# Head layout of three sixteen-head attention stages: copies within SBUF in place of a trip through DRAM

## The chip, the cores and the metric

The kernel runs on one core of a Trainium2 chip. The metric is the device time of one execution in microseconds. Three executions took 2805.46, 2811.95 and 2813.29 us (median 2811.95). The traces and tables show one further, profiled execution, which took 2811.11 us; its span from the first to the last instruction is 2809.3 us.

## The reference

A decoder of eleven stages works on 8 sequences of 256 tokens with 256 channels (2048 tokens), with a context of 120 tokens a sequence. Four stages are attention with 16 heads of 16 channels. For each of them the reference is, in short:

```
q = (x @ Wq + bq), k = (source @ Wk + bk), v = (source @ Wv + bv)   # 256 channels = 16 heads of 16
p = softmax(q_h . k_h / 4 + mask)        # for each head h
x = layernorm(x + concat_h(p @ v_h) @ Wo + bo)
```

L0a attends over tokens mixed across sequences, L1a is causal with rotary embedding, L1x attends over the context (120 keys a sequence), L2a is causal with keys and values from a latent of 64 channels. The other seven stages (cross attention, experts, product keys, feed-forward) are not touched.

## The kernel before, in words

Activations lie transposed in SBUF, channels on the 128 partitions, tokens along the row. The stages run one after the other, and each is built from blocks. A block ends in a barrier over all engines, so that nothing of the next block starts before the slowest engine of this one is through; the wait that SP (SyncE) makes at the end of its program counts as well.

`heads_stage` builds the four sixteen-head stages (L0a, L1a, L1x, L2a). Its first block projects. TensorE makes Q in four chunks of 512 tokens, two halves of 128 channels each, ScalarE copies each half from PSUM to `Qc` (L1118), then TensorE makes K in chunks (four of 512; in L1x two of 480) and VectorE copies these to `Kc` (L1142), then V (L1098, L1150). `Qc` and `Kc` are compact: head h lies on 16 rows starting at 16(h mod 8), in half h div 8. The score matmuls of the next block want each head at the start of a 32-row group: the padded tiles `Q` and `K` have four groups of rows (head mod 4, rows 32i to 32i+15) by four planes (head div 4), and the other 16 rows of a group hold a constant that GpSimd (L1033) and VectorE (L1123) write beforehand.

Moving the heads from compact to padded is SP's work in this first block. For each chunk `put_heads` stores it to DRAM in one transfer over all 128 partitions (L980, 512 KB), and `take_heads` waits until that store has landed and loads it back in four transfers of 128 KB, each into 16 rows by four planes (L992). The store of a chunk is issued ahead of the loads of the chunk before it; the two semaphores `put0` and `put1` take turns. After the last chunk SP waits for all loads (L1013, L1014; in L0a also L1016) and only then reaches the barrier. L1a, with rotation, has a store in two transfers instead of one (L977) and is otherwise alike.

The second block computes scores for the row maximum, the third scores again, exponentials and values. There the results go from padded back to compact rows by copies within SBUF, 16 rows by 512 tokens and 32 KB each in L0a and L1x (L1310, half of them issued by SP, half by ScalarE's queue). These are the only copies of that kind in the kernel before.

Of the kernel before, what the change touches and what calls it, by code (L numbers as in the profile page):

```python
# [18 lines left out]
P = 128  # L19
# [3 lines left out]
DH = D // P  # L23
# [109 lines left out]
NCH = T // CH  # L133
# [780 lines left out]
HD, HEADS, HP, G4 = 16, 16, 32, 4  # L914


def heads_stage(nc, c, name):

    a = HEADS16[name]
    s, w, ps = c.sig, c.w[name], c.psum  # L920
    kv, keys, mix, rope = a["kv"], a["keys"], a.get("mix"), a.get("rope")
# [5 lines left out]
    KCH, KCHN = (B * CTX // 2, 2) if ctx_keys else (CH, NCH)  # L927
# [4 lines left out]
    with ExitStack() as ctx:  # L932
        def sb(nm, shape, dt=F32, where=ctx):
            return where.enter_context(nc.sbuf_tensor(f"{name}_{nm}", shape, dt))

        Q = sb("Q", [P, G4, T])
        K = sb("K", [P, G4, B * KTOK])
# [6 lines left out]
        def padded_rows(h):  # L944
            return slice(HP * (h % 4), HP * (h % 4) + HD)

        def compact_rows(h):
            return slice(HD * (h % 8), HD * (h % 8) + HD)

        with ExitStack() as part:  # L950
            lat = sb("lat", [P, 1, T], F32, part) if kv == "lat" else None
            R = sb("R", [P, 2, DH, CH], F32, part) if rope else None
            Qc = sb("Qc", [P, DH, T], F32, part)
            Kc = sb("Kc", [P, DH, B * KTOK], F32, part)
# [5 lines left out]
            items = [("q", n, CH) for n in range(NCH)], [("k", n, KCH) for n in range(KCHN)]  # L960
            if rope:
                items = [x for pair in zip(*items) for x in pair]
            else:
                items = items[0] + items[1]

            PUTS = 16 * DH if rope else 16

            def put_heads(sp, slot, kind, n, width):
                cols = slice(n * width, (n + 1) * width)
                if rope:  # L970
                    sp.wait_ge(s["rope_add"].sem, s["rope_add"].at(2 * n + (1 if kind == "q" else 2)))
                else:
                    sp.wait_ge(s[f"{kind}_evac"].sem, s[f"{kind}_evac"].at(DH * (n + 1)))
                whole = Qc if kind == "q" else Kc
                if rope:
                    for j in range(DH):
                        sp.dma_start(c.heads[kind][:, cols].rearrange("(h j i) t -> j h i t", j=DH, i=HD // 2)[j],  # L977
                                     whole[:, j, cols]).then_inc(s[f"put{slot}"].sem, 16)
                else:
                    sp.dma_start(c.heads[kind][:, cols].rearrange("(j p) t -> p j t", p=P), whole[:, :, cols])\  # L980
                        .then_inc(s[f"put{slot}"].sem, 16)

            def take_heads(sp, slot, turn, kind, n, width):
                cols = slice(n * width, (n + 1) * width)
                sp.wait_ge(s[f"put{slot}"].sem, s[f"put{slot}"].at(PUTS * turn))
                if kind == "q":
                    sp.wait_ge(s["q_clear"].sem, s["q_clear"].at(n // 2 + 1))
                else:
                    sp.wait_ge(s["k_clear"].sem, s["k_clear"].at(1))
                stored = c.heads[kind][:, cols].rearrange("(g i d) t -> i d g t", i=4, d=HD)  # L990
                for i in range(4):
                    sp.dma_start((Q if kind == "q" else K)[padded_rows(i), :, cols], stored[i]).then_inc(s[f"laid_{kind}"].sem, 16)  # L992

            with nc.Block() as block:  # L994
                @block.sync
                def _(sp):

                    if mix:
                        own = c.ins["xpT"].rearrange("(j p) t -> p j t", p=P)
                        c.load_first(sp)  # L1000
                        sp.dma_start(xp[:, :, 0:CH], own[:, :, 0:CH]).then_inc(s["tile0"].sem, 16)
                        c.load(sp, 0, PACK[name][0]["bk"][0])
                        for n in range(1, NCH):
                            sp.dma_start(xp[:, :, n * CH:(n + 1) * CH], own[:, :, n * CH:(n + 1) * CH]).then_inc(s[f"tile{n}"].sem, 16)
                        c.load_base(sp)
                    c.prefetch(sp, name)
                    for i, item in enumerate(items):
                        put_heads(sp, i % 2, *item)
                        if i:
                            take_heads(sp, (i - 1) % 2, (i + 1) // 2, *items[i - 1])  # L1010
                    i = len(items) - 1
                    take_heads(sp, i % 2, i // 2 + 1, *items[i])
                    sp.wait_ge(s["laid_q"].sem, s["laid_q"].at(64 * NCH))  # L1013
                    sp.wait_ge(s["laid_k"].sem, s["laid_k"].at(64 * KCHN))  # L1014
                    if mix:
                        sp.wait_ge(c.loaded.sem, 16 * 4)  # L1016

# [140 lines left out]
            counts = dict(v_proj=B * VT, v_evac=B * VT, w_first=16 if mix else 0, padded_v=1, q_clear=2, k_clear=1)  # L1158
            if mix:
                counts.update({f"tile{n}": 16 for n in range(NCH)})  # L1160
            counts.update(laid_q=64 * NCH, laid_k=64 * KCHN, put0=PUTS * ((len(items) + 1) // 2), put1=PUTS * (len(items) // 2))
            if rope:
                counts.update(rope_proj=2 * NCH, rope_mul=2 * NCH, rope_add=2 * NCH)
            else:
# [130 lines left out]
        with ExitStack() as part:  # L1295
# [4 lines left out]
            width = 3 * P if keys == "causal" else CH  # L1300
# [2207 lines left out]
def program(nc, ins, out):  # L3508
    c = Core()
    with ExitStack() as ctx:  # L3510
# [106 lines left out]
        for name in run:  # L3617
            if name in HEADS16:
                heads_stage(nc, c, name)
            elif name in ATTENTION:  # L3620
                attention_stage(nc, c, name)
            else:
                OTHER[name](nc, c, ins)
# [132 lines left out]
```

## Time and profile before

| | |
|---|---|
| median of three runs | 2811.95 us |
| profiled execution | 2811.11 us, span 2809.3 us |
| TensorE matmul busy | 2139.6 us (76%) |
| VectorE busy | 1704.1 us (61%) |
| ScalarE busy | 955.7 us (34%) |
| GpSimd busy | 850.2 us (30%) |
| first block of L0a | 0 to 68 us |
| first block of L1x | 850 to 894 us |
| first block of L2a | 1333 to 1395 us |

A busy share over the whole span says little here, since the eleven stages have different limits. What counts for a change to one block is which engine or queue of that block reaches the barrier last, and how long the others have then been idle. The granted clock of TensorE averages 0.877 of full speed.

### The profile page before, as it was taken

Reading aid. Unit: us, or ns where it says so; the run is one execution under the profiler, and the core shown is the slowest. Engines: PE = TensorE matmul, PEld = TensorE weight load, DVE = VectorE, ACT = ScalarE, POOL = GpSimd, SP = SyncE. Lnnn points to the kernel's source line nnn. Section 1 sums busy time; section 2 is a strip of 40 time slices with the busy share of each in tenths; the row PEclk is TensorE's granted clock in tenths of the full one; section 3 lists DMA queues with packets and bytes.
Section 4 is the critical chain, followed back from the end, with each engine's and each line's share of the span. In section 5 each row is a group of like instructions: output and inputs, shape, how many; then the busy total and the mean of one; then the engine's idle time right before and its main releaser. Section 6 shows DMA issues by size and latency. Waiting matters only on the chain. (4 is left out here: it accounts for less than half of the span.)

```text
span 2809.3 us, 37739 instructions
## 1 busy us (share of the span) xinstructions
PE 2139.6 (76%) x13417; PEld 1415.7 (50%) x13417; DVE 1704.1 (61%) x4445; ACT 955.7 (34%) x1774; POOL 850.2 (30%) x807
## 2 busy tenths in 40 slices
PE   6887679876887775684679685778787788668796
PEld 3544459834543442572355333666676666535332
DVE  3754411176654768445485676678888877536586
ACT  0142324310351331232105464344454444335343
POOL 1001032250001007451100002777777777303000
PEclk8999679988998876897799898888898988889898
DMA  8210057437007134653601204422222222130000
GB/s 232 67 26 3 25 186 264 141 93 198 13 20 182 51 125 162 215 187 134 120 2 28 78 1 126 109 60 65 59 61 61 59 67 62 41 88 1 0 0 30
DMA packets 133770, 241.88 MB, mean 86 GB/s; under 512 B 41824, under 2 KB 78816, under 8 KB 127080
## 3 DMA queue, kind: packets, MB, share of 16 engines
q1 hardware_dynamic: 69887, 128.53, 15.9%
q0 software_dynamic: 56416, 102.76, 11.8%
q10 hardware_dynamic: 7296, 8.40, 1.0%
q8 instruction: 97, 1.59, 0.2%
q14 instruction: 74, 0.60, 0.1%
HBM read 267.00 MB, written 69.73 MB: 120 GB/s over the span
## 5 line engine op out<-in xcount | busy, mean ns | idle before, releaser
L3000 POOL DMA_INDIRECT L2f_G<-in_L2f_table,L2f_idx x512 | 530.2, 1036 | 174.2 <-issue 153.6
L3351 DVE CUSTOM_DVE_ANT_0 L2f_junk<-L2f_G,L2f_X 128x256 bf16<-128x256 f32 x512 | 182.7, 421 | 131.8 <-DMA L2f_G<-in_L2f_table,L2f_idx 131.5
L3075 PE MATMUL psum<-L2f_G,L2f_diag 128*128 128x256 f32 x768 | 188.2, 397 | 0.0
L3075 PEld LDWEIGHTS psum<-L2f_G,L2f_diag 128*128 128x128 f32 x768 | 152.0, 201 | 34.2 <-issue 7.3
L1192 PE MATMUL psum<-constb 128*128 128x256 bf16 x512 | 91.4, 284 | 74.7 <-PEq L994 39.8
L3052 PE MATMUL psum<-xT,L2f_mw 128*128 128x256 f32 x512 | 135.2, 412 | 11.9 <-DVE L2f_h L3357 11.9
L2350 POOL DMA_INDIRECT picks_x<-L1f_rows,L1f_put x64 | 71.3, 1114 | 207.4 <-DVE L1f_sm L2563 188.2
L3215 ACT ACTIVATE L2f_diag<-const,L2f_actd 128x128 f32<-128x128 f32 x400 | 123.9, 389 | 29.9 <-DVE L2f_actd L3365 29.9
L3052 PEld LDWEIGHTS psum<-xT,L2f_mw 128*128 128x128 f32 x512 | 106.7, 210 | 30.9 <-DVE L2f_h L3357 13.1
L3208 ACT ACTIVATE L2f_actd<-L2f_dots 128x9 f32<-128x9 f32 (+1 forms) x64 | 13.5, 210 | 285.6 <-DVE L2f_dots L3351 285.6
L1192 PEld LDWEIGHTS psum<-constb 128*128 128x128 bf16 x512 | 40.8, 99 | 131.3 <-issue 59.9
L3062 PE MATMUL psum<-L2f_h,L2f_mw 128*128 128x256 f32 x256 | 74.5, 418 | 41.4 <-DVE L2f_acc L3401 41.4
L1371 ACT ACTIVATE L1a_PT<-psum 128x1536 f32<-128x1536 f32 x32 | 46.4, 1451 | 169.8 <-PE psum L1341 169.8
L1719 ACT ACTIVATE L0f_h<-psum,L0f_wu 128x128 f32<-128x128 f32 x184 | 57.6, 364 | 97.6 <-PE psum L1693 97.6
L1693 PEld LDWEIGHTS psum<-L0f_xeT,L0f_wu 128*128 128x128 f32 x736 | 88.3, 197 | 2.1 <-issue 1.0
L1693 PE MATMUL psum<-L0f_xeT,L0f_wu 128*128 128x128 f32 x736 | 88.5, 280 | 0.6 <-DVE L0f_xeT L1727 0.6
L2704 POOL DMA_INDIRECT picks_y<-L1f_ye,L1f_home x64 | 62.0, 969 | 73.6 <-ACT L1f_ye L2769 61.0
L1705 PE MATMUL psum<-L0f_wd,L0f_h 128*128 128x256 f32 x368 | 83.2, 379 | 0.0
L1862 PE MATMUL psum<-L3f_h,weights 128*128 128x512 f32 x128 | 65.6, 660 | 22.4 <-DVE L3f_h L1933 22.4
L2124 POOL TENSOR_TENSOR L2x_room<-L2x_Fu 128x256 f32<-128x256 f32 x8 | 5.6, 722 | 253.8 <-ACT L2x_Fu L2134 253.7
L3062 PEld LDWEIGHTS psum<-L2f_h,L2f_mw 128*128 128x128 f32 x256 | 53.0, 210 | 52.2 <-issue 44.3
L1705 PEld LDWEIGHTS psum<-L0f_wd,L0f_h 128*128 128x128 f32 x368 | 68.1, 190 | 8.3
(671 smaller groups left out, 5036.4 us busy)
## 6 DMA issues: line engine op xcount, KB each, us to landing
L1f_we<-in_L1f_w SPq DMA_DIRECT2D x32, 384.0 KB, 9.7
picks_x<-zeros SPq DMA_DIRECT2D x16, 544.0 KB, 8.7
L1f_xe<-picks_x SPq DMA_DIRECT2D x32, 272.0 KB, 2.8
picks_y<-zeros SPq DMA_DIRECT2D x16, 512.0 KB, 6.5
L2f_G<-in_L2f_table,L2f_idx POOLq DMA_INDIRECT x512, 2.8
slots_x<-zeros POOLq DMA_DIRECT2D x8, 512.0 KB, 7.6
L1f_wb<-in_L2x_w SPq DMA_DIRECT2D x1, 4096.0 KB, 12.1
L1f_g<-picks_y SPq DMA_DIRECT2D x8, 512.0 KB, 13.1
```

The costliest lines, as they stand in the source:

```text
L1192: nc.tensor.matmul(out, c.one, m.broadcast_to([P, 2, P]), start=True, stop=False, skip_group_check=True)
L1693: mm = nc.tensor.matmul(ps[:, f // 2, (f % 2) * TILE:(f % 2 + 1) * TILE], wu[:, k, j * F + f * P:j * F + f * P + P], xeT[:, k, j, :], star ...
L1705: mm = nc.tensor.matmul(ps[:, 6 + k, 0:D], h[:, k, f, :], wd[:, k, f * D:(f + 1) * D], start=(f == 0), stop=(f == FT - 1))
L1862: mm = nc.tensor.matmul(ps[:, 4 + 2 * (n % 2) + o, :], w["w2"][:, f * D + o * P:f * D + o * P + P], h[:, u % 2, i * CH:(i + 1) * CH], star ...
L2350: nc.gpsimd.indirect_dma_start(out=c.picks_x[:, :], out_offset=bass.IndirectOffsetOnAxis(ap=put[:, t, k:k + 1], axis=0), in_=rows[:, t, :] ...
L2704: nc.gpsimd.indirect_dma_start(out=c.picks_y[:, :], out_offset=bass.IndirectOffsetOnAxis(ap=home[:, e % NB, q:q + 1], axis=0), in_=ye[:, e ...
L3000: nc.gpsimd.indirect_dma_start(out=G[:, h, k, :], out_offset=None, in_=ins["L2f_table"], in_offset=bass.IndirectOffsetOnAxis(ap=IDX[:, t, ...
L3052: mm = nc.tensor.matmul(ps[:, UP + i % 2, chunk(g)], wt[:, j * F + f * P:j * F + f * P + P], c.xT[:, j, chunk(k)], start=(j == 0), stop=(j ...
L3062: mm = nc.tensor.matmul(ps[:, DOWN, chunk(o_)], wd[:, f * D + o_ * P:f * D + o_ * P + P], h_[:, i % 3, :], start=(f == 0 and o_ == 0), sto ...
L3075: mm = nc.tensor.matmul(ps[:, MIX + t % 2, 0:D], diag[:, i % 2, k, :], row[:, D:2 * D], start=(h == 0 and k == 0), stop=(h == HEADS - 1 an ...
L3215: e = nc.scalar.activation(diag[:, i % 2, k, :], c.ident, ACT.Copy, scale=act_d[:, i % 2, k:k + 1])
L3351: e = VE.tensor_tensor_reduce(out=junk[:, k, :], in0=row[:, 0:D], in1=X[:, t % 3, :], scale=1.0, scalar=0.0, op0=ALU.mult, op1=ALU.add, ac ...
```

## The change

In the stages without rotation (L0a, L1x, L2a) the store to DRAM and the four loads of a chunk are replaced by eight transfers straight from the compact tile to the padded one. For each i of 0 to 3 and each parity 16 rows of `Qc` by two halves by 512 tokens go to rows 32i of `Q`, in planes 0 and 2 or in planes 1 and 3: 32 pieces of 2 KB, 64 KB a transfer. The wait for the store's semaphore is gone; the waits for the copies out of PSUM and for the cleared padding stay, and stand ahead of the eight transfers. The counts at the end of the block follow (128 a chunk instead of 64). L1a is as before.

```diff
+            LAID = 64 if rope else 128
+            PUTS = 16 * DH if rope else 0
+
+            def lay_heads(sp, kind, n, width):
+                cols = slice(n * width, (n + 1) * width)
+                whole, padded = (Qc, Q) if kind == "q" else (Kc, K)
+                if kind == "q":
+                    sp.wait_ge(s["q_clear"].sem, s["q_clear"].at(n // 2 + 1))
+                else:
+                    sp.wait_ge(s["k_clear"].sem, s["k_clear"].at(1))
+                sp.wait_ge(s[f"{kind}_evac"].sem, s[f"{kind}_evac"].at(DH * (n + 1)))
+                for i in range(4):
+                    for odd in range(2):
+                        sp.dma_start(padded[padded_rows(i), odd::2, cols], whole[compact_rows(4 * odd + i), :, cols])\
+                            .then_inc(s[f"laid_{kind}"].sem, 16)
...
-                    for i, item in enumerate(items):
-                        put_heads(sp, i % 2, *item)
-                        if i:
-                            take_heads(sp, (i - 1) % 2, (i + 1) // 2, *items[i - 1])
-                    i = len(items) - 1
-                    take_heads(sp, i % 2, i // 2 + 1, *items[i])
-                    sp.wait_ge(s["laid_q"].sem, s["laid_q"].at(64 * NCH))
-                    sp.wait_ge(s["laid_k"].sem, s["laid_k"].at(64 * KCHN))
+                    if rope:
+                        for i, item in enumerate(items):
+                            put_heads(sp, i % 2, *item)
+                            if i:
+                                take_heads(sp, (i - 1) % 2, (i + 1) // 2, *items[i - 1])
+                        i = len(items) - 1
+                        take_heads(sp, i % 2, i // 2 + 1, *items[i])
+                    else:
+                        for item in items:
+                            lay_heads(sp, *item)
+                    sp.wait_ge(s["laid_q"].sem, s["laid_q"].at(LAID * NCH))
+                    sp.wait_ge(s["laid_k"].sem, s["laid_k"].at(LAID * KCHN))
```

SP's program in the first block of L0a, before: from the last load of weights to the third chunk of Q. L980 is the store, L992 the loads, and a row with "waits" names the semaphores ahead of it.

```order
L3553 DMA weights<-in_w_L0x 128x1796
L980 DMA heads_q<-L0a_Qc 128x2x512 [waits q_evac] x2
L992 DMA L0a_Q<-heads_q 16x4x512 [waits q_clear,put0]
L992 DMA L0a_Q<-heads_q 16x4x512 x3
L980 DMA heads_q<-L0a_Qc 128x2x512 [waits q_evac]
L992 DMA L0a_Q<-heads_q 16x4x512 [waits q_clear,put1]
L992 DMA L0a_Q<-heads_q 16x4x512 x3
```

The same place after the change (L979 is the new copy, L3564 the load of weights):

```order
L3564 DMA weights<-in_w_L0x 128x1796
L979 DMA L0a_Q<-L0a_Qc 16x2x512 [waits q_evac,q_clear]
L979 DMA L0a_Q<-L0a_Qc 16x2x512 x7
L979 DMA L0a_Q<-L0a_Qc 16x2x512 [waits q_evac,q_clear]
L979 DMA L0a_Q<-L0a_Qc 16x2x512 x7
L979 DMA L0a_Q<-L0a_Qc 16x2x512 [waits q_evac,q_clear]
```

Five transfers and two kinds of wait for each chunk have become eight transfers behind one wait, and no transfer waits for another any more.

The end of SP's program in the first block of L2a, before, with the last two chunks of K and the wait that leads to the barrier:

```order
L992 DMA L2a_K<-heads_k 16x4x512 x3
L980 DMA heads_k<-L2a_Kc 128x2x512 [waits k_evac]
L992 DMA L2a_K<-heads_k 16x4x512 [waits k_clear,put0]
L992 DMA L2a_K<-heads_k 16x4x512 x3
L992 DMA L2a_K<-heads_k 16x4x512 [waits k_clear,put1]
L992 DMA L2a_K<-heads_k 16x4x512 x3
L994 UNCONDITIONAL_BRANCH [waits laid_k,laid_q]
```

And after:

```order
L979 DMA L2a_K<-L2a_Kc 16x2x512 [waits k_evac,k_clear]
L979 DMA L2a_K<-L2a_Kc 16x2x512 x7
L979 DMA L2a_K<-L2a_Kc 16x2x512 [waits k_evac,k_clear]
L979 DMA L2a_K<-L2a_Kc 16x2x512 x7
L1001 UNCONDITIONAL_BRANCH [waits laid_k,laid_q]
```

The last store and the wait for it have left the end of the block; sixteen copies stand where one store and eight loads stood. The other engines' programs keep their order.

## Rows read from the trace of the kernel before

**Rows 1.** The page's first line.

```profile
span 2809.3 us, 37739 instructions
```

**Rows 2.** Timeline around the end of L0a's first block: start, duration, engine, line.

```profile
50.55 0.42 DVE L1150 TENSOR_TENSOR L0a_V<-psum,weights 128x256 f32<-128x256 f32 x1 [0.44 <-PE psum L1098]
...
67.98 1.87 PE L1195 MATMUL psum<-constb 128*128 128x512 bf16 x4 [17.47 <-PEq L994]
```

**Rows 3.** The same around the end of L1x's first block.

```profile
886.19 0.16 DVE L247 TENSOR_TENSOR weights<-weights,L1x_mid 128x2 f32<-128x2 f32 x1
...
893.98 1.43 PE L1251 MATMUL psum<-L1x_K,L1x_Q 32*128 32x120 f32 x18 [10.27 <-PEq L994]
```

**Rows 4.** The same for L2a.

```profile
1372.71 0.16 DVE L247 TENSOR_TENSOR weights<-weights,L2a_mid 128x2 f32<-128x2 f32 x1
...
1395.00 1.01 PE L1192 MATMUL psum<-constb 128*128 128x256 bf16 x4 [24.77 <-PEq L994]
```

**Rows 5.** SP's queue: what it waited for at the three block ends (L0a, L1x, L2a).

```profile
SPq L1016 <- DMA L0a_K<-heads_k: 5.4, 1, 5.4
...
SPq L1014 <- DMA L1x_K<-heads_k: 6.5, 1, 6.5
...
SPq L1014 <- DMA L2a_K<-heads_k: 6.4, 1, 6.4
```

**Rows 6.** SP's queue in L2a: first stores, and loads of the last chunks of K.

```profile
1346.91 3.80 SPq L980 DMA_DIRECT2D heads_q<-L2a_Qc  x2
...
1370.71 1.72 SPq L992 DMA_DIRECT2D L2a_K<-heads_k  x4
...
1375.96 1.71 SPq L992 DMA_DIRECT2D L2a_K<-heads_k  x4
...
1386.39 1.71 SPq L992 DMA_DIRECT2D L2a_K<-heads_k  x4
```

**Rows 7.** SP's queue in L0a: first stores, first loads, last loads.

```profile
13.60 3.62 SPq L980 DMA_DIRECT2D heads_q<-L0a_Qc  x2
26.16 1.74 SPq L992 DMA_DIRECT2D L0a_Q<-heads_q  x4
...
60.36 1.71 SPq L992 DMA_DIRECT2D L0a_K<-heads_k  x4
```

**Rows 8.** SP's queue in L1x: first stores, first loads, last loads.

```profile
856.43 3.80 SPq L980 DMA_DIRECT2D heads_q<-L1x_Qc  x2
...
860.34 2.22 SPq L992 DMA_DIRECT2D L1x_Q<-heads_q  x4
...
884.91 1.71 SPq L992 DMA_DIRECT2D L1x_K<-heads_k  x4
```

**Rows 9.** Windows: busy time by engine, TensorE clock, DMA share, GB/s.

```profile
1346.90:1350.50 3.60, 3.60 (x10) 1.67 (x9) 0.00 (x0) 1.38 (x2) 0.00 (x0) 1.00 0.38 146
...
1368.00:1378.00 10.00, 2.23 (x11) 1.61 (x9) 4.69 (x12) 0.00 (x0) 0.00 (x0) 0.74 1.06 210
...
13.00:26.00 13.00, 13.00 (x32) 5.82 (x31) 0.75 (x1) 4.70 (x7) 0.19 (x1) 1.00 1.02 411
```

**Rows 10.** Copies within SBUF, L1x: issue ns, time to landing, one window with four.

```profile
L1310 SPq DMA_DIRECT2D L1x_ATc<-L1x_Q x32: 507/586/962, 955.6 to 999.6; - x32
...
DMA to landing us min/median/max: 1.9/2.2/2.7
...
958.00:961.00 3.00, 2.79 (x33) 1.37 (x32) 2.15 (x5) 1.88 (x1) 0.00 (x0) 1.00 0.21 44
```

**Rows 11.** Copies out of PSUM: ns min/median/max, first and last start.

```profile
L1118 ACT ACTIVATE L2a_Qc<-psum,weights x8: 688/688/688, 1344.5 to 1356.5; 128x512 f32<-128x512 f32 x8
...
L1142 DVE TENSOR_SCALAR L0a_Kc<-psum,weights x8: 751/751/751, 24.8 to 36.7; 128x512 f32<-128x512 f32 x8
L1142 DVE TENSOR_SCALAR L2a_Kc<-psum,weights x8: 750/750/751, 1357.4 to 1363.4; 128x512 f32<-128x512 f32 x8
```

**Rows 12.** GB/s in 40 slices of 1381 to 1394, the last loads of L2a.

```profile
GB/s 177 183 151 189 246 189 170 120 113 183 303 347 290 202 107 76 76 69 63 113 240 164 139 114 120 113 120 126 126 88 76 63 57 82 95 50 19 0 0 0
```

**Rows 13.** Issues of the loads of Q in L1x: ns of one issue, min/median/max.

```profile
L992 SPq DMA_DIRECT2D L1x_Q<-heads_q x16: 302/426/821, 860.3 to 875.5; - x16
```

More of the change, by code:

```diff
@@ L964, in heads_stage @@
                 items = items[0] + items[1]
-            PUTS = 16 * DH if rope else 16
+            LAID = 64 if rope else 128
[12 more added lines that the diff above has]
+                            .then_inc(s[f"laid_{kind}"].sem, 16)
             def put_heads(sp, slot, kind, n, width):
                 cols = slice(n * width, (n + 1) * width)
[L970 to L973, printed above, removed]
+                sp.wait_ge(s["rope_add"].sem, s["rope_add"].at(2 * n + (1 if kind == "q" else 2)))
                 whole = Qc if kind == "q" else Kc
[L975 to L981, printed above, removed]
+                for j in range(DH):
+                    sp.dma_start(c.heads[kind][:, cols].rearrange("(h j i) t -> j h i t", j=DH, i=HD // 2)[j],
+                                 whole[:, j, cols]).then_inc(s[f"put{slot}"].sem, 16)
             def take_heads(sp, slot, turn, kind, n, width):
@@ L1160, in heads_stage @@
                 counts.update({f"tile{n}": 16 for n in range(NCH)})
-            counts.update(laid_q=64 * NCH, laid_k=64 * KCHN, put0=PUTS * ((len(items) + 1) // 2), put1=PUTS * (len(items) // 2))
+            counts.update(laid_q=LAID * NCH, laid_k=LAID * KCHN, put0=PUTS * ((len(items) + 1) // 2), put1=PUTS * (len(items) // 2))
             if rope:
```

## The prediction, made before the changed kernel was timed

> **What bounds the kernel now.** The page's first line gives the scale: a span of 2809.3 us inside an execution of 2811.11 us, so 1.8 us lie outside the span [rows 1]. Shares of busy time over the whole program say nothing about this edit, so I read the timeline at the three block ends that it touches. In L0a the last compute instruction, a copy of V out of PSUM, ends at 50.97, and the first matmul of the next block starts at 67.98 [rows 2]. In L1x VectorE ends at 886.35 and the next matmul starts at 893.98 [rows 3]; in L2a 1372.87 and 1395.00 [rows 4]. So the engines stand idle for 17.0, 7.6 and 22.1 us. What they wait for is in SP's own waits: at each end SP waits 5.4 to 6.5 us for the last loads of K to land [rows 5], after having issued them late. Adding the wait to the end of the last issues in L2a gives 1386.39 + 1.71 + 6.4 = 1394.5, half a microsecond ahead of the next matmul. The three blocks end with the head transfers, and the most that the change can give is about those gaps.
>
> Then the question is what sets the pace of these transfers. In L2a the loads of successive K chunks are issued 5.25 us apart (1370.71, 1375.96, then two more to 1386.39) [rows 6], and the windows say why: between 1368 and 1378 the sixteen DMA engines are fully occupied (share 1.06) while they move 210 GB/s [rows 9]. In L0a the loads from the inputs move 411 GB/s at the same share [rows 9]. So the head traffic fills the DMA engines, at half the rate that they can do. It is not the latency of store and load alone that costs.
>
> **What one chunk costs before.** A round is one store plus four loads, 1.05 MB in 5.25 us. The first store of L2a stands nearly alone in the window from 1346.9 to 1350.5: 3.6 us at a share of 0.38 is 1.37 us of the DMA engines [rows 9]. That leaves 5.25 − 1.37 = 3.9 us for the four loads, whose 512 KB all go to 16-row groups. The block ends confirm it, since there the loads of two chunks run with no store left: from the moment that the last store has landed to the landing of everything it takes 62.07 + 5.4 − 60.36 = 7.1 us in L0a [rows 5, 7], 886.62 + 6.5 − 884.91 = 8.2 us in L1x [rows 5, 8] and 1388.10 + 6.4 − 1386.39 = 8.1 us in L2a [rows 5, 6]. Halved, that is 3.55 to 4.1 us for a chunk that goes into padded rows.
>
> **What one chunk costs after.** The change removes the store (1.37 us of the engines) and the wait for it. It writes the same 512 KB to the same padded rows, now in eight transfers of 64 KB whose source is SBUF. Two things can set the pace:
> - The transfer itself. If the writing side decides, as the loads show, a chunk takes 3.55 to 4.1 us. The nearest rows for the new kind of copy are the 32 KB copies of the third block: four of them in 3.0 us occupy the DMA engines at a share of 0.21, so 0.63 us for four [rows 10]. A chunk is sixteen times 32 KB, 2.5 us: that is the lower bound, with the copies far apart and little in each other's way.
> - The issue by SP. A copy of this kind takes 507 ns at the least and 586 ns in the median on SP's queue [rows 10], with ScalarE's queue issuing at the same time; the loads before take 302 to 426 ns [rows 13]. Eight issues are 8 × 0.55 = 4.4 us with the first pair of numbers, 3.4 us with 0.426.
>
> The copies out of PSUM don't hold it up. ScalarE's in L2a are 1.7 us apart (eight from 1344.5 to 1356.5), a chunk of Q each 3.4 us, and K is complete by 1364.2 there and by 37.5 in L0a [rows 11], each long before SP gets to its last chunk. Where SP can work from an idle queue (L1x, L2a) I take the issue, 4.4 us a chunk. In L0a the DMA engines are behind: the first store, issued at 13.60, has landed only at 26.16 [rows 7], against 860.34 − 856.43 = 3.9 us on the idle queue of L1x [rows 8]. The transfers there begin as if issued at 26.16 − 3.9 = 22.3, by which time SP would have issued two chunks, so that the transfer decides and not the issue; I take the upper end of its own bounds, 4.1 us, since the pieces are as large but the transfers twice as many. Behind the last issue stand the landing of a small copy, 1.9 us [rows 10], and 0.5 us through the barrier, as found above: 2.4 us.
>
> **The sum.**
> - L0a: 22.3 + 8 × 4.1 + 2.4 = 57.5, against 67.98: 10.5 us less.
> - L1x, six chunks: 856.4 + 6 × 4.4 + 2.4 = 885.2, which is ahead of VectorE's end at 886.35. So VectorE is late next, the block ends at 886.35 + 0.5 = 886.9, and the gain is 7.1 us of 7.6.
> - L2a: 1346.9 + 8 × 4.4 + 2.4 = 1384.5, against 1395.00: 10.5 us less. TensorE's and VectorE's work ends at 1372.87, so the transfers still decide.
>
> Together 28.1 us. The wait that moves, for the copies out of PSUM and the cleared padding, has only SP's own transfers behind it; nothing else is queued there, since the prefetch of the next weights is issued ahead. L1a keeps its way. The next blocks start from a barrier, so everything behind shifts as a whole; what the DMA queue does later (filling of the pick tables, the copies back to compact rows) keeps its distance from the block start. TensorE's clock has fallen to its lower level in the idle stretches and will still have done so in L0a and L2a; I count nothing for it. From the profiled 2811.11 us that gives 2783.0 us. The median of the runs shown is 0.8 us above the profiled execution, which I leave out: 2783.
>
> **A rule weighed.** The rows say that loads into 16-row groups run at 512 KB in 3.55 to 4.1 us, so 128 to 148 GB/s, against 411 GB/s of the wide loads [rows 5 to 9]. The Trainium skill, page SBUF — State Buffer, section "Door 1: The DMA port swizzle", says that the bandwidth goes by how many of sixteen ports the partitions reach, 27.2 GB/s each, four partitions in a row sharing one. Sixteen rows reach four ports, 109 GB/s, and an estimate from that is 4.8 us a chunk when one transfer runs at a time; by it the sum would be 4.9 + 6.4 + 7.3 = 18.6 us and the time 2792.5. The trace is faster than that rule read for one transfer, and I take it that transfers into different row groups overlap.
>
> **The rivals.**
> 1. *In step.* Successive transfers go to the same row group (four of them, then the next pair of groups), so all sixteen DMA engines may press on the same few rows, now on the reading side too, with no wide store between to spread them. For it speaks that in the last loads of L2a the rate has stretches of 57 to 126 GB/s [rows 12]; at 107 GB/s, one slice of it, a chunk costs 4.9 us. SP at over 0.6 us an issue would give the same. Then L0a ends at 22.3 + 39.2 + 2.4 = 63.9 (4.1 less), L1x at 888.2 (5.8 less), L2a at 1388.5 (6.5 less): 16.4 us, time 2794.7. Against it: the averages of 3.55 to 4.1.
> 2. *Slower: both sides narrow.* Before, a byte was read from SBUF in a wide transfer and written in a narrow one. Now both ends of each transfer are 16 rows, and if reading and writing don't overlap, a chunk costs twice 3.85, 7.7 us. Then L0a ends at 86.3 (18.3 later), L1x at 905.0 (11.0 later), L2a at 1410.9 (15.9 later): 45 us more, time 2856. The change breaks even at 5.64 us a chunk over the 22 chunks, 0.70 us a transfer; above that it loses. Against it speak the copies of the third block, narrow on both sides, which land in 1.9 to 2.7 us with 0.16 us of the engines each [rows 10]; for it, that they never came eight in a row. A size rule points the same way: the Trainium skill, page DMA: Bandwidth & Descriptors, section "Bandwidth", asks for transfers of 1 MiB and gives 0.95 us for 64 KB one at a time. An estimate from it is 7.6 us a chunk and 2854 us; no row here shows 64 KB copies.
> 3. *Hidden whole.* If the chunk costs under 3.3 us (the lower bound is 2.5, and SP issues at 0.4 us), the compute ends decide everywhere: L0a at 51.5, L2a at 1373.4, and the gain is 16.5 + 7.1 + 21.6 = 45.2 us, time 2765.9. The issue time speaks against it.
> 4. *About even.* A chunk between 5.26 and 6.0 us leaves the time within 8.4 us of the old one; it would be half of rival 2.
>
> **How the numbers follow.** Likeliest is my sum, a chunk of 3.55 to 4.6 us: 0.54. Rival 1: 0.22. Rival 3: 0.05. Rival 4: 0.07. Rival 2: 0.12. At 3.55 us everywhere the gains are 14.9 + 7.1 + 17.3 = 39.3 and the time 2771.8; the slow end of rival 1, 5.26 us a chunk, is 2802.7. I take 2771 to 2802 as the range; outside it lie most of rivals 2 and 3 and a part of 4. Faster by over 0.3% (8.4 us, about what the measurement can tell from no change) is my sum with rivals 1 and 3: 0.81. Within 0.3%: 0.07. Slower: 0.12.
>
> **What would show it.** In the profile after: the first matmul behind each of the three blocks at about 57.5, 876 (886.9 less the 10.5 of L0a) and 1367 (1384.5 less 17.6). SP's issues of the new copy at 0.5 to 0.6 us. SP's wait at the end of the L2a block down from 6.4 to about 2 us if the issue decides, still 4 us or more if the transfers do. No gap between VectorE's last instruction and the barrier of L1x beyond 0.5 us; L1a's block as long as before. The forecast is wrong if the DMA share stays at 1 with under 110 GB/s (rivals 1 and 2), if an issue of the new copy costs over 0.6 us, or if the blocks gain as computed and a later stage gives time back.

## The result, and the profile after

The changed kernel took 2799.46 us in the median of five runs (2798.20 to 2806.19), the kernel before 2811.95 us beside it. The ratio is 0.9961 (95% interval 0.9943 to 0.9979). A second set of runs later gave 2794.84 against 2810.25 us, ratio 0.9940 (0.9924 to 0.9955). The medians differ by 12.5 and 15.4 us, where 28 us were forecast. The range of 2771 to 2802 held the median, but the gain was about half of what the sum gave. The profiled execution was the slowest of its five, 2806.19 us.

The page's first line of the kernel after, which answers to [rows 1]:

```profile
span 2804.4 us, 37799 instructions
```

The timeline at the three block ends, after. The columns are those of [rows 2 to 4], and the lines answer to them one by one (L0a, L1x, L2a):

```profile
51.53 0.42 DVE L1161 TENSOR_TENSOR L0a_V<-psum,weights 128x256 f32<-128x256 f32 x1 [0.44 <-PE psum L1109]
59.70 1.01 PE L1206 MATMUL psum<-constb 128*128 128x512 bf16 x2 [8.21 <-PEq L1001]
...
880.83 0.16 DVE L247 TENSOR_TENSOR weights<-weights,L1x_mid 128x2 f32<-128x2 f32 x1
...
884.91 3.78 PE L1262 MATMUL psum<-L1x_K,L1x_Q 32*128 32x120 f32 x64 [6.56 <-PEq L1001]
...
1365.86 0.16 DVE L247 TENSOR_TENSOR weights<-weights,L2a_mid 128x2 f32<-128x2 f32 x1
...
1384.52 1.01 PE L1203 MATMUL psum<-constb 128*128 128x256 bf16 x4 [21.13 <-PEq L1001]
```

The idle ends are 7.8, 3.9 and 18.5 us long now, against 17.0, 7.6 and 22.1 before. The head copies still decide all three blocks, L1x included, where VectorE was to be last.

SP's queue, after, in L0a and L2a, each row a run of issues with its start and length (compare [rows 6, 7]), and the durations of one issue:

```profile
14.45 21.13 SPq L979 DMA_DIRECT2D L0a_Q<-L0a_Qc  x32
35.68 21.79 SPq L979 DMA_DIRECT2D L0a_K<-L0a_Kc  x32
...
1340.11 21.24 SPq L979 DMA_DIRECT2D L2a_Q<-L2a_Qc  x32
1361.45 20.75 SPq L979 DMA_DIRECT2D L2a_K<-L2a_Kc  x32
...
L979 SPq DMA_DIRECT2D L2a_K<-L2a_Kc x32: 585/592/598, 1361.4 to 1381.6; - x32
```

There is no gap between these runs of issues: SP issues from the first chunk to the last. An issue lasts 592 ns, and the next starts 0.65 us after its start (20.2 us from the first to the last start, over 31 steps). Eight are 5.2 us, the length of a round before; the two agree by chance, since a round was set by the full DMA engines. SP's waits at the block ends, which answer to [rows 5], and L2a's window with the share and GB/s of the DMA engines in its last columns ([rows 9]):

```profile
SPq L1027 <- DMA L0a_K<-L0a_Kc: 1.7, 1, 1.7
...
SPq L1025 <- DMA L1x_K<-L1x_Kc: 1.7, 1, 1.7
...
SPq L1025 <- DMA L2a_K<-L2a_Kc: 1.8, 1, 1.8
...
1341.00:1384.00 43.00, 22.38 (x69) 12.56 (x67) 14.54 (x29) 4.12 (x6) 0.00 (x0) 0.81 0.61 98
```

The last copy has landed 1.7 us after its issue ends, so nothing is queued up, and the DMA engines are busy 61% at 98 GB/s where they were full at 210. As read here, the bound has moved from the transfers to SP's issue; the experiments test it.

For the rest of this text a block is measured from the start of its stage to VectorE's clearing of the next block's tile, less than a microsecond behind the barrier. The rest of the span is everything outside the four first blocks.

| kernel | L0a | L1a | L1x | L2a | rest of the span |
|---|---|---|---|---|---|
| before | 68.9 | 59.1 | 44.8 | 63.3 | 2573.2 |
| before, second profile | 69.4 | 59.2 | 44.6 | 62.7 | 2580.8 |
| after | 60.6 | 59.9 | 41.6 | 58.2 | 2584.1 |
| after, second profile | 60.4 | 59.9 | 40.8 | 59.4 | 2574.2 |

The three blocks gave 8.7 + 3.5 + 4.2 = 16.4 us on the average of the two profiles, and L1a, which the change does not reach, was 0.8 longer. That is within its scatter: in the thirteen profiles of kernels with the same L1a it takes 57.3 to 60.3 us. Of the 16.4 us the first two profiles show only 4.9 in their spans, since the rest of the span after is 10.9 us longer.

### The profile page after: what moved, and what is told of

It is laid out like the page before. It is cut to its first block and busy times, and to the rows that moved or that the text cites. A ratio compares the mean times of both kernels' runs of the same rounds, so it can differ in the third digit from the quotient of the medians.

```text
span 2804.4 us, 37799 instructions
## 1 busy us (share of the span) xinstructions
PE 2149.9 (77%) x13411; PEld 1424.0 (51%) x13417; DVE 1705.4 (61%) x4445; ACT 954.5 (34%) x1774; POOL 849.2 (30%) x807
## 5 line engine op out<-in xcount | busy, mean ns | idle before, releaser
L3073 PEld LDWEIGHTS psum<-L2f_h,L2f_mw 128*128 128x128 f32 x256 | 53.4, 212 | 50.9 <-issue 42.8
L1044 POOL MEMSET L1x_Q<- 128x4096 f32 x2 | 7.0, 3511 | 216.8 <-POOLq L1414 216.8
```

Of the source, the lines that this page charges most:

```text
L3073: mm = nc.tensor.matmul(ps[:, DOWN, chunk(o_)], wd[:, f * D + o_ * P:f * D + o_ * P + P], h_[:, i % 3, :], start=(f == 0 and o_ == 0), sto ...
```

## The experiments

Two terms are used below. *Theory A* is that the issue decides, with a copy each 0.65 us on a queue. Its rivals are *theory B*, that the narrow transfers need as long anyway, and, for what was missing in the first profile, that the edit slows later stages.

**K's copies on ScalarE's queue.** They stand in ScalarE's program behind its last copy of Q out of PSUM.

```diff
-                        for item in items:
+                        for item in items[:NCH]:
                             lay_heads(sp, *item)
...
+                        for item in items[NCH:]:
+                            lay_heads(nc.scalar, *item)
```

> The copies of Q stay on SyncE's queue, those of K go to ScalarE's, behind its last copy of Q out of PSUM. Nothing else changes; the same 64 copies of 64 KB. Theory A, the issue decides (one copy each 0.65 us on a queue): in L0a Q is issued from 14.5 to 35.3 and K beside it from 27.2 to 48.0, everything has landed by 50 and the compute end at 51 decides, so the first matmul of the next block stands at 51.5 instead of 59.7. In L2a Q takes 21 us from 1340 and K from 1352 to 1373, so the block ends about 9 us earlier than after the change. L1x gains 2 to 3 us and ends at VectorE's end. Together 19 us less than the changed kernel, some 2780. Theory B, the transfers themselves need about 5 us a chunk on narrow rows (in step): the second queue changes nothing, under 2 us, and the last wait grows from 1.8 us to 8 or more. Between the two, at 3.6 to 4.1 us a chunk: L2a ends at about 1374 instead of 1384.5 by transfers as well.

It took 2780.10 us, ratio 0.9906 (0.9887 to 0.9925); blocks 56.0, 37.5 and 52.0 us (L0a, L1x, L2a). L1x is at VectorE's end. The same copies with the same bytes gained 4.5, 3.7 and 6.8 us against the means of the changed kernel by being issued from two queues. That is 15.0 us of the 19 expected, so that the median of 2780 came out as forecast only with some luck. B as stated falls, but A is not the whole of it, as a window in L0a shows:

```profile
24.00:54.50 30.50, 25.97 (x93) 17.27 (x91) 12.79 (x24) 0.00 (x0) 0.00 (x0) 1.00 1.03 135
```

With the issue out of the way the DMA engines are full at 135 GB/s, 3.9 us a chunk, and L0a still ends 4 us behind its compute work. In L2a, however, the issue decides again, now on ScalarE's queue:

```profile
1341.01 22.27 ACTq L979 DMA_DIRECT2D L2a_K<-L2a_Kc  x32
```

These 32 issues are 0.70 us apart and end at 1363.28, and SP's wait for the last landing ends 1.9 us later.

**Two chunks a copy.**

```diff
-                cols = slice(n * width, (n + 1) * width)
+                cols = slice(n * 2 * width, (n + 1) * 2 * width)
...
-                        for item in items:
-                            lay_heads(sp, *item)
+                        for kind, n, width in items:
+                            if n % 2 == 0:
+                                lay_heads(sp, kind, n // 2, width)
```

> All on SyncE's queue, but each copy takes two chunks at once (16 rows by 2 halves by 1024 tokens, 128 KB), so half as many issues for the same bytes; the first copy has to wait for the second chunk, 3.4 us later. Theory A with the cost by issue and not by bytes: an issue stays at 0.6 to 0.65 us, SyncE needs 5.2 us for two chunks, the queue gets to the end soon after the last copy out of PSUM and then the transfers are late: at 3.6 to 4.1 us a chunk L2a's block ends 8 to 10 us earlier than after the change, L0a's 5 to 8 us, time some 2785. If the issue costs by bytes (1.2 us each), or theory B (5 us a chunk) holds, the blocks end where they do after the change or 3 us later, about 2800 or more.

The waits and counts follow the wider copies. It took 2792.24 us, ratio 0.9943 (0.9925 to 0.9961); blocks 60.2, 39.7, 56.0, where gains of 5 to 8 us in L0a and 8 to 10 in L2a were expected. An issue of 128 KB and a window in L2a:

```profile
L979 SPq DMA_DIRECT2D L2a_K<-L2a_Kc x16: 585/600/1246, 1343.0 to 1353.8; - x16
...
1345.00:1365.00 20.00, 5.48 (x26) 4.46 (x24) 7.88 (x20) 0.00 (x0) 0.00 (x0) 0.75 1.05 120
```

The issue costs 600 ns for twice the bytes: by transfer, not by byte. But now the transfers decide, at 120 GB/s, 4.4 us a chunk: the last issue of L2a ends at 1354.42 and SP waits another 14.5 us. The 4.4 us are more than the 3.55 to 4.1 us that the loads of before took, and most of what halving the issues would have given is lost to it.

**Each copy in two.** The inner loop issues the two halves of channels apart, 16 copies of 32 KB a chunk.

> Each copy is cut in two by the halves of channels: 16 copies of 32 KB a chunk, same bytes, all on SyncE. Theory A: issue at 0.51 to 0.59 us plus 0.06 us each, 9.2 to 10.4 us a chunk, so the first block of L2a grows from 57 us to 57 + 8 x (4 to 5.2) = 89 to 99 us, L0a's from 59.7 to 90 or more. Theory B or a cost by bytes: 0.33 us an issue, the blocks as after the change.

One run of 2889.81 us; blocks 98.3, 70.4 and 97.5, and the last wait 1.4 us. An issue takes 589 ns for 32 KB. Twice the issues lengthened L2a by 39 us and L0a by 38, which is 0.6 us for each of the 64 more issues, as A has it; from start to start they are 0.64 us apart.

**Only L2a changed.**

> Only L2a has the direct copies, L0a and L1x keep the way by DRAM. If the block gains add and nothing gives them back, L2a's first block is 5.1 us shorter (57.3 instead of 62.4 us) and the time 5 us lower, 2807. The blocks of the changed kernel gave 8.3 + 3.3 + 5.1 = 16.7 us and the median fell by 12.5; if the clock's low stretches scatter by some microseconds from run to run and from kernel to kernel, other stages here differ from before by 1 to 3 us each in both directions, without a pattern tied to the edit; if the edit itself slows later stages, L2a's second block or L2x is longer again, by 2 us or more.

It took 2811.15 us, ratio 0.9991 (0.9975 to 1.0007), which cannot be told from no change; 5 us less were expected. L2a's block is 59.2 us, 4 us shorter as in the changed kernel, but the rest of the span in its profile is 2584.2 us. The interval has room for a gain of 7 us, so this run shows the block and says nothing on the time.

**Row groups in turn.** This is the kernel with two chunks a copy, in another order. The question is whether neighbouring copies limit each other (theory C) or each is limited by its own 16 rows (theory D).

```diff
-                for i in range(4):
-                    for odd in range(2):
+                for odd in range(2):
+                    for i in (0, 2, 1, 3):
```

> The copies of two chunks on SyncE's queue (the kernel with 8 copies of 128 KB for two chunks), issued in another order: row groups 0, 2, 1, 3 for one parity and then for the other, in place of each group twice in a row. Same copies, same bytes. In that kernel the queue is behind, the DMA engines are full (share 0.98) at 114 GB/s in L2a, 4.6 us a chunk. Theory C, neighbouring copies into the row groups 0 and 1 share what limits them, and 2 and 3 share another, so that they run in step: alternating lets one go beside the other, the rate rises to 140 GB/s or more, L2a's block falls from 56.0 us to 50 or less, L0a's from 60.2 to 56 or less. Theory D, each copy is limited by its own 16 rows, whatever its neighbour: the rate stays at 114 to 120 GB/s and the blocks within 1 us of the kernel compared.

2774.27 us, ratio 0.9872 (0.9856 to 0.9888), the fastest median of all; blocks 54.4, 38.2, 51.5. In L2a:

```profile
1345.00:1358.00 13.00, 5.26 (x25) 4.27 (x23) 7.68 (x19) 0.00 (x0) 0.00 (x0) 0.79 1.05 142
```

142 GB/s against 120 at the same full share, by order alone: theory C holds in its direction. L2a's block missed the 50 us by 1.5. The new order changes two things at once, which rows of `Q` and `K` neighbouring copies write and which rows of the compact tile they read; the kernel before, two runs further on, has only the first.

**The same order on the changed kernel.** One queue, 64 KB copies.

> The changed kernel, its 64 copies on SyncE's queue alone, in alternating order. The issue limits it at 0.65 us a copy, so faster transfers give nothing: blocks of 60.5, 41 and 58.5 us within 1 us, last wait 1.7 to 1.9 us. If transfers had been the limit it would gain 5 us in L0a and in L2a.

One run of 2800.35 us; blocks 60.3, 41.6, 58.6, last waits 1.7 to 1.8 us. The order that gives 6 and 4.5 us (L0a, L2a) where the transfers decide gives nothing here. That is the plainest evidence that the changed kernel is bound by SP's issue. It is not that the order did nothing to these copies. In L0a they queue up behind the input loads at first, and there the same window reads as follows in the changed kernel and in this one:

```profile
24.00:30.00 6.00, 6.00 (x15) 2.66 (x14) 2.25 (x3) 0.67 (x1) 0.00 (x0) 1.00 1.08 135
...
24.00:30.00 6.00, 6.00 (x15) 2.66 (x14) 2.74 (x4) 0.00 (x0) 0.00 (x0) 1.00 1.09 198
```

The same 64 KB copies from one queue moved at 135 GB/s (116 in the second profile of the changed kernel) and at 198 GB/s. With the backlog gone the issue set the pace in both.

**The same order on the kernel before.** `take_heads` loops over (0, 2, 1, 3), in all four stages; nothing else is edited.

> The kernel before, by DRAM, with the four loads of a chunk in the order 0, 2, 1, 3 of row groups (L1a's too). If neighbouring row groups 0 and 1, 2 and 3 share what limits the writing side, here too a chunk's loads go faster: a round falls from 5.25 us to 4.5 or less, the blocks of L0a and L2a from 68.9 and 63.3 to 63 and 57, L1x and L1a by 2 to 5 us, time 10 to 18 us lower than before. If the alternation helped only because of the copies' reading side, nothing moves by more than 1 us.

It took 2789.84 us against 2814.21, ratio 0.9921 (0.9893 to 0.9948), where 10 to 18 us less were expected; blocks 64.0, 53.5, 40.5, 54.5 (L1a second). A pair of loads in L2a and a window there, to compare with [rows 6, 9]:

```profile
1351.50 1.72 SPq L992 DMA_DIRECT2D L2a_K<-heads_k  x4
...
1355.85 1.71 SPq L992 DMA_DIRECT2D L2a_K<-heads_k  x4
...
1350.00:1362.00 12.00, 3.53 (x17) 2.75 (x15) 5.97 (x15) 0.00 (x0) 0.00 (x0) 0.84 1.03 251
```

A round is 4.35 us instead of 5.25, at 251 GB/s instead of 210. The loads read from DRAM, so the order acts on the writing side. Four numbers in a loop, with the way by DRAM kept, gave 24 us in the medians and 23.5 us in the four blocks. Of these 5.6 us are in L1a, which the change does not reach; in the three blocks that it does reach the order gave 17.9 us against the change's 16.4. The intervals of the two ratios overlap.

**Both queues in that order**, with 64 KB and with 128 KB copies, and with SP taking the last chunk of K.

> Q issued by SyncE, K by ScalarE's queue, copies of 64 KB, in the order 0, 2, 1, 3 of row groups. The kernel without the new order had blocks of 56.0 (L0a), 37.5 (L1x) and 52.0 us (L2a) and still waited for landings. Theory C: in L0a the compute end at 51 decides, block 52 us; L2a's block 46 to 48 us, with the last issue of K by ScalarE at 34 us from the block's start. L1x is at VectorE's end and stays. Time 4 to 9 us under the 2780 of that kernel, some 2774. Theory D: the same blocks within 1 us, time 2780.

> Both queues, two chunks a copy, alternating order: the issue is 0.6 us for 128 KB on two queues and limits nothing; the transfers alone decide. Under theory C the blocks are near those of the kernel with 64 KB copies on two queues and alternating order, perhaps 1 to 3 us longer since each copy starts one chunk (3.4 us) later. Under theory D L2a's block is 52 to 56 us.

> Both queues, copies of 64 KB in alternating order, and SyncE takes the last chunk of K besides Q; ScalarE's queue has the other chunks of K. If what is left in L2a is the issue (ScalarE's queue ends its 32 copies 48 us after the start of the block), SyncE's last eight end at 41 and ScalarE's 24 at 43, and L2a's block falls from 51.3 to 47 us; L0a (53.0) and L1x (37.9) are at the ends of their compute work, 52 to 53 and 37.7, and stay. Time 3 to 5 us under 2780, some 2775. If the transfers decide, at 3.6 us a chunk from 16 us on, the block is 47 as well, at 4.2 us a chunk 51 and no gain.

They took 2779.71 (0.9899, 0.9881 to 0.9917), 2775.38 (0.9875, 0.9858 to 0.9892) and 2781.40 us (0.9896, 0.9863 to 0.9928). Blocks in the order of the table, without L1a: 53.0, 37.9, 51.3; 53.0, 38.8, 53.8; 53.4, 37.7, 51.7. L0a and L1x stand at their compute ends, L0a to within 0.5 us. L2a did not follow. With 64 KB copies (first run) its end is that of the issues on ScalarE's queue, as without the new order. With SP's help (third run) the issues end at 1347 and the DMA engines are full:

```profile
1339.00:1351.00 12.00, 3.22 (x15) 2.47 (x14) 5.67 (x14) 0.00 (x0) 0.00 (x0) 0.73 1.11 133
```

This is 133 GB/s although the order alternates, and in the first run 132 GB/s from 1344 to 1350. It may be that two queues mix their copies, so that the order on the row groups is lost; that is my reading and was not tested. It cannot be the whole, since in L0a the first run moved 199 GB/s from 24 to 39 us with both queues at work from 28 on, against 141 without the new order. What makes the difference between the two stages stays open. The intervals of these three and of the fastest kernel overlap.

**Second profiles.**

> The changed kernel once more, to narrow its time and for a second profile. The first blocks of L0a, L1x and L2a should be 60.6, 41.6 and 58.2 us again within 0.5 us. Everything else of the span was 2584.1 us in its first profile and 2573.2 us in the one of the kernel before. If that difference of 10.9 us belongs to the change, this profile has 2582 to 2586 us there again; if it is scatter between executions, it has anything from 2562 to 2585, and the median of many runs falls by about the 16.7 us that the three blocks gave, less or more by a few.

> The kernel before once more, for a second profile. The four first blocks should be 68.9, 59.1, 44.8 and 63.3 us again within 0.5 us; the rest of the span, 2573.2 us in its first profile, may be anything from 2562 to 2585 if it scatters between executions as in the other kernels.

The blocks came out within 1.2 us of the first profiles, where 0.5 was expected, and the rest of the span at 2574.2 and 2580.8 us. Over all fourteen profiles it runs from 2562.5 to 2584.2. Two profiles of one kernel differ by 7.6 us (before) and 9.9 us (after), and the kernel with only L2a changed has the longest rest. The longer rest of the first profile after is within this scatter; a price of a few microseconds could not be seen in it, but none shows in the second set of runs.

## Why the prediction was wrong

- *What bounds the kernel* was right. The three idle ends were the head transfers, and the gain came out of them.
- *What one chunk costs after: the issue by SP* is the step that failed. The term was 8 × 0.55 = 4.4 us and measured 5.2. I had taken the mean of the shortest and the median duration of the 32 KB copies [rows 10] and left out the 0.06 us from the end of one issue to the start of the next. The 592 to 593 ns of the new copy is near the median of 586 that stood there. Over eight chunks that is 6.4 us in L2a, and 4.8 us over the six of L1x, which turned its end from VectorE's to SP's. The run with 32 KB copies (+38 and +39 us), the one with K on a second queue (15 us gained) and the one where a faster order gained nothing show that this term is the bound.
- *In L0a the transfer decides* was wrong in kind, by the same term. The DMA engines are full until about 42 us there (share 0.98 from 39 to 42, 0.54 in the next 3 us) and have then worked off what the input loads left; SP issues without pause from 14.45 to 57.47, and the last copy waits 1.7 us. The two chains to compare are 22.3 + 8 × 4.1 = 55.1 for the transfers and, with 4.4 us a chunk, 14.45 + 35.2 = 49.7 for the issues. At the measured 0.67 us an issue the second ends at 57.5. The gain was 8.3 us in that profile for 10.5.
- *The transfer itself*, 3.55 to 4.1 us a chunk, was about right and hidden behind the issue. Where copies of 64 KB are uncovered it is 3.9 us: in L0a from 24 to 30 us at 135 GB/s (4.5 in the second profile, at 116), and with two queues. With two chunks a copy it is 4.4 us, and in alternating order it is less, 2.6 us at 198 GB/s.
- *The sum* from the measured blocks is 16.4 us for 28.1. With 5.2 us a chunk in place of 4.4 and 4.1 and the start at 22.3 in L0a left as it was, the sum of the prediction would have been 1.7 + 4.0 + 4.1 = 9.8 us; the start at 22.3, which holds for landings and not for issues, had put the end of L0a 7.9 us too late, and the chunk's cost had put it 10.2 us too early (8 × (5.38 − 4.1)), so that the two errors hid each other in part. What the medians show, 12.5 and 15.4, agrees with 16.4 less L1a's 0.8 within their intervals.
- *The rule weighed*: by the Trainium skill, page SBUF — State Buffer, section "Door 1: The DMA port swizzle", partitions 32 apart share a port and partitions 64 apart do not. Applied here, row groups 0 and 1 share ports, and so do 2 and 3, and the two runs with alternating order agree: 120 to 142 GB/s and 210 to 251 GB/s. I had read from it only the rate of one transfer and had not worked out what it means for neighbours. The 198 GB/s in L0a are above the 109 GB/s that I had worked out from it for 16 rows, so transfers into different row groups do overlap.
- *The rivals*: the first, "in step", with 4.9 us a chunk and 2794.7 us, is the nearest to what happened. It named both causes, SP at over 0.6 us an issue and neighbours in step; the runs show the first at work and the second right behind it. It had a chance of 0.22. That its total of 16.4 us is also the measured one is luck: it had 4.1, 5.8 and 6.5 us for L0a, L1x and L2a, and measured are 8.7, 3.5 and 4.2. Rival 2, narrow ends on both sides, had 7.7 us a chunk; measured are 3.9 to 4.5, and the estimate of 7.6 us from the size of the transfers fell with it. In rival 3 the condition was misread: L2a is hidden whole only under 3.0 us a chunk ((1373.4 − 2.4 − 1346.9) / 8), not 3.3.
- *A gain that later stages give back* is not shown. The profile scatters outside the blocks by more than the blocks gained. A part is TensorE's granted clock, seen in the same stretch of L1a's second block (the clock is the number ahead of the last two, 0.95 and 0.90 of full speed), before and after:

```profile
661.00:737.00 76.00, 59.48 (x732) 37.08 (x732) 68.75 (x70) 1.45 (x1) 0.00 (x0) 0.95 0.39 118
```

```profile
652.70:728.70 76.00, 60.64 (x707) 37.51 (x705) 68.54 (x70) 0.00 (x0) 0.00 (x0) 0.90 0.39 119
```

L1a as a whole took 248.6 and 251.0 us there. What sets the clock's phase in one execution stays open.

## What to carry to other kernels

When a few wide transfers become many narrow ones, count the issuing queue first: the interval from start to start of the nearest like instruction, times the number, is a bound of its own and does not shrink with the bytes. When the DMA engines are full below their rate, look at which rows neighbouring transfers touch before changing the route; here an order of row groups alone, with the way through DRAM kept, gave at least as much as the change of route did (17.9 against 16.4 us in the same three blocks). And a gain of half a per cent is read from the blocks that the edit touches, since the rest of the span can scatter by more than that.

## What the runs showed of the hardware that was not expected

An issue of a copy within SBUF took 589 to 600 ns in the median on SP's queue at 32, 64 and 128 KB alike, and a load from DRAM into the same 16-row groups 426 ns [rows 13]. Copies of 128 KB that go to the same row group and then to the one 32 rows on ran at 120 GB/s, those alternating with groups 64 rows apart at 142, and copies of 64 KB, in L0a, at 116 to 135 and at 198, with the sixteen DMA engines fully busy all four times; busy engines are no sign that the rate is at its limit.
